# A cross-attention and expert layer on one core: projections, the gate and the turns of the output stand in other iterations

## The reference

```python
def attention(x, cross_input, ...):             # B, T, TC, C, H = 8, 512, 1024, 256, 16
    q, k, v = heads(x @ Wq + bq), heads(x @ Wk + bk), heads(x @ Wv + bv)
    att = where(causal, einsum('bhqd,bhkd->bhqk', q, k) * scale, -inf)
    y = softmax(att) @ v
    qc = heads(x @ Wcq + bcq)
    kc, vc = heads(cross_input @ Wck + bck), heads(cross_input @ Wcv + bcv)
    y = y + softmax(qc @ kc^T * scale) @ vc
    return y @ Wp + bp

def experts(x, gate_w, ...):                    # x: 4096 tokens
    scores = (tanh(x @ gate_w.T) + 1) * 0.5
    vals, idx = top_k(scores.T, 512)            # per expert
    h = gelu(einsum(layernorm(x[idx]), fc1s) + b1s)
    return x.at[idx].add((einsum(h, fc2s) + b2s) * vals)

x = x + attention(layernorm(x), ctx, ...)
x = x + experts(layernorm(x), ...)
```

## Time and profile before

| | |
|---|---|
| median of 3 runs | 1535.83 us (1532.77 to 1536.47) |
| the profiled execution | 1536.36 us, its span 1534.6 us |
| TensorE busy (matmul) | 1433.9 us, 93% |
| VectorE busy | 1167.2 us, 76% |
| ScalarE busy | 899.4 us, 59% |
| GpSimd busy | 551.7 us, 36% |
| mean granted clock of TensorE | 0.963 |
| DMA | 155.21 MB, mean 101 GB/s |

### The profile page before, as it was taken

One profiled execution on the slowest core, in us unless ns is written; L12 is line 12 of the kernel. 1 busy time (PEld: TensorE's weight loads), 2 busy tenths in 40 slices (PEclk: granted clock), 3 DMA queues, 4 the chain that ended last, 5 costly groups with the idle time before them and its releaser, 6 DMA issues. The chain is left out here.

```text
span 1534.6 us, 25472 instructions
## 1 busy us (share of the span) xinstructions
PE 1433.9 (93%) x8558; PEld 690.1 (45%) x8560; DVE 1167.2 (76%) x3025; ACT 899.4 (59%) x1753; POOL 551.7 (36%) x1015
## 2 busy tenths in 40 slices
PE   8899999999999999999999999999998947999997
PEld 4443343444344434444443444344443323766674
DVE  6879888988898888889888988898894176455441
ACT  2067777777777777777777777777777401112111
POOL 4032234341444144423534341443113122454452
PEclk9599999999999999999999999999999877999998
DMA  6884666738482947485566738392800120444442
GB/s 177 113 143 88 96 104 135 91 85 126 120 119 68 151 110 95 98 175 88 89 123 149 93 83 125 107 120 73 132 3 3 42 88 20 123 101 117 128 94 51
DMA packets 82387, 155.21 MB, mean 101 GB/s; under 512 B 13008, under 2 KB 46416, under 8 KB 82256
## 3 DMA queue, kind: packets, MB, share of 16 engines
q1 hardware_dynamic: 74752, 142.43, 49.0%
q0 software_dynamic: 6144, 8.52, 3.3%
q10 hardware_dynamic: 1360, 2.62, 0.5%
HBM read 96.52 MB, written 53.08 MB: 97 GB/s over the span
## 5 line engine op out<-in xcount | busy, mean ns | idle before, releaser
L850 ACT ACTIVATE probs<-bank_ps 128x512 f32<-128x512 f32 (+1 forms) x1408 | 721.6, 581 | 226.4 <-PE bank_ps L640 222.4
L956 DVE TENSOR_REDUCE chunk_max<-bank_ps 128x1 f32<-128x512 f32 x1024 | 652.0, 682 | 85.8 <-PE bank_ps L679 80.7
L640 PE MATMUL bank_ps<-q_stack,k_stack 64*128 64x512 f32 (+3 forms) x1536 | 507.2, 420 | 45.4 <-ACT probs L850 43.8
L679 PE MATMUL bank_ps<-k_stack,q_stack 62*128 62x512 f32 (+3 forms) x1536 | 525.4, 431 | 9.5 <-DMA k_stack<-parts 4.4
L679 PEld LDWEIGHTS bank_ps<-k_stack,q_stack 62*128 62x128 f32 x1536 | 248.4, 190 | 359.7 <-DVE chunk_max L956 235.3
L1165 POOL TENSOR_TENSOR pool_idle<-pool_idle 128x1 f32<-128x1 f32 x293 | 56.7, 194 | 757.6 <-ACT probs L850 520.7
L640 PEld LDWEIGHTS bank_ps<-q_stack,k_stack 64*128 64x128 f32 x1536 | 237.1, 187 | 128.2 <-ACT probs L850 125.2
L658 PE MATMUL out_ps<-probs,v_cross 128*32 128x512 f32 x2048 | 275.3, 610 | 0.0
L959 DVE CUSTOM_DVE_ANT_0 masked<-bank_ps,causal 128x128 bf16<-128x128 f32 (+3 forms) x512 | 232.0, 484 | 56.8 <-PE bank_ps L679 54.9
L1503 ACT ACTIVATE h<-h_ps,b1T 128x512 f32<-128x512 f32 x64 | 44.0, 687 | 226.9 <-PE h_ps L1435 224.9
L1435 PE MATMUL h_ps<-ff_yT,w1T 128*128 128x512 f32 x256 | 113.0, 595 | 0.6 <-DVE ff_yT L1516 0.6
(11 more groups left out here) (173 smaller groups left out, 1329.6 us busy)
## 6 DMA issues: line engine op xcount, KB each, us to landing
parts_dram<-parts SPq DMA_DIRECT2D x70, 512.0 KB, 2.7
k_stack<-parts_dram SPq DMA_DIRECT2D x180, 192.0 KB, 14.4
q_stack<-parts_dram SPq DMA_DIRECT2D x180, 128.0 KB, 13.3
w1T<-in_L_ffn_fc1s SPq DMA_DIRECT2D x8, 1024.0 KB, 5.6
w2T<-in_L_ffn_fc2s SPq DMA_DIRECT2D x8, 1024.0 KB, 7.4
z_rows<-z_sb SPq DMA_DIRECT2D x8, 528.0 KB, 14.3
x_sb<-in_x SPq DMA_DIRECT2D x8, 512.0 KB, 4.4
ctxT<-in_ctx SPq DMA_DIRECT2D x8, 512.0 KB, 14.1
```

What stands on the lines that cost most here:

```text
L640: mm = pe.matmul(bank_of(turn)[:, of.at:of.end], k_stack[base:base + SIDE, g, pair, of.keys:of.keys + P], q_stack[base:base + SIDE, g, pai ...
L679: return pe.matmul(bank[:, 0:n], q_stack[base:base + MAX_ROWS, g, pair, qc:qc + P], k_stack[base:base + MAX_ROWS, g, pair, k0:k0 + n], sta ...
L850: nc.scalar.activation(probs[:, buffer(u, i, p), side, columns], bank_of(("score", g, i, p, side))[:, columns], ACT.Exp, scale=SCALE)\
L956: nc.vector.tensor_reduce(dst, bank[:, 0:n], AX.X, ALU.max).then_inc(max_done, 1)
```

## The change

Two tables are changed, and nothing else: the place of twelve pieces and of seven outputs. All work is the same, and so are the loops that read the tables.

```diff
@@ PLAN, L71 @@
-    (0, 7): (("shift", 0),), (0, 8): (("k", 0),), (0, 9): (("q", 0),), (0, 10): (("kc1", 0),), (1, 1): (("qc", 0),),
-    (1, 2): (("kc0", 0),), (1, 7): (("shift", 0), ("proj0", 0)), (2, 1): (("proj1", 0),), (2, 2): (("q", 1),),
-    (2, 5): (("vc0", 0),), (2, 6): (("vc1", 0),), (2, 7): (("shift", 0),), (2, 8): (("zT0", 0),),
-    (2, 10): (("zT1", 0),), (3, 0): (("kc1", 1),), (3, 2): (("qc", 1),), (3, 3): (("k", 1),), (3, 4): (("kc0", 1),),
-    (3, 6): (("v", 0),), (3, 7): (("shift", 0),), (3, 8): (("gate", 0),),
+    (0, 7): (("shift", 0),), (0, 9): (("qc", 0),), (0, 10): (("kc1", 0),), (1, 1): (("q", 0),), (1, 2): (("k", 0),),
+    (1, 3): (("kc0", 0),), (1, 7): (("shift", 0), ("proj0", 0)), (2, 1): (("proj1", 0),), (2, 2): (("q", 1),),
+    (2, 3): (("vc1", 0),), (2, 7): (("shift", 0),), (2, 8): (("kc1", 1),), (2, 10): (("zT0", 0),),
+    (3, 0): (("vc0", 0),), (3, 2): (("qc", 1),), (3, 3): (("kc0", 1), ("zT1", 0)), (3, 4): (("k", 1),),
+    (3, 6): (("v", 0),), (3, 7): (("shift", 0), ("gate", 0)),
@@ OUTPUT_PLAN, L79 @@
-    (0, 1): ("turn_cross",), (0, 2): ("divide_cross",), (0, 6): ("turn_self",), (0, 8): ("divide_self",),
+    (0, 1): ("turn_cross",), (0, 2): ("divide_cross",), (0, 3): ("turn_self",), (0, 5): ("divide_self",),
...
-    (1, 3): ("divide_self",), (2, 1): ("turn_cross",), (2, 2): ("divide_cross",), (2, 4): ("turn_self",),
-    (2, 5): ("divide_self",), (3, 2): ("turn_back",), (3, 4): ("turn_cross",), (3, 5): ("divide_cross", "turn_self"),
-    (3, 8): ("divide_self",),
+    (1, 3): ("divide_self",), (2, 1): ("turn_cross",), (2, 2): ("divide_cross", "turn_self"),
+    (2, 8): ("divide_self",), (3, 2): ("turn_back",), (3, 3): ("turn_cross",), (3, 4): ("divide_cross",),
+    (3, 5): ("turn_self",), (3, 6): ("divide_self",),
```

## The result

| | before | after |
|---|---|---|
| median (lowest to highest) | 1534.51 us (1531.16 to 1538.76) | 1539.38 us (1533.46 to 1547.87) |
| runs, on the same chip | 20 | 20 |
| ratio, 95% interval | | 1.0036 [1.0024, 1.0047] |
| profiled execution | 1536.36 us | 1533.84 us, span 1532.1 |
| TensorE busy | 1433.9 us | 1428.4 us |

The change makes the kernel 0.36% slower, 4.9 us between the medians. The profiled execution of after happens to be one of its shortest (1533.84 where the median is 1539.38), so this trace alone would have suggested a gain. What makes a run long has therefore to be found from several profiles.

A forecast was written before the change was run, and what follows sets the result against it. TensorE, busy 93% of the span, was taken as the bound. Middle batches -1.7 us, batch 0 0, batch 7 -0.5 and batch 1's slow stretch -0.2 gave -2.4, a median of 1533.5 us; range 1528.5 to 1539.0.

The forecast's parts named there:

- (0, 8): Iteration 8 of unit 0: loses projection k, from 4.20 us to a bare slot of 2.62, -1.58 a middle batch.
- (1, 3): Iteration 3 of unit 1: bare at 2.69 us, gets kc0 and takes 3.18, +0.49 a middle batch.
- (3, 3): Iteration 3 of unit 3: gets kc0 and zT1 for k, -0.23 us a middle batch.
- (3, 7): Iteration 7 of unit 3: gate joins the shift, +1.30 us on 3.33; bank wait bounded by 0 and +0.2.
- -0.28: Sum of all slot entries in a middle batch, in us, with 0.4 either way.
- rival 2: Gate waits 0.2 for its bank, VectorE late at (2, 2), (2, 8): +0.1 to +0.3 a batch, 1536-1537 us; chance 0.2.
- Queues passed: GpSimd and SyncE queues: splits, stores and fills of moved pieces stay covered, cost 0; lost cover under 1 us a batch.
- I leave the number of falls as it is: TensorE's clock drops to its lower level at gates as often as before; one costs 1.13 us in a middle batch.
- Rival 3: Shift and gate in a row make the clock fall at (3, 7) every middle batch: 1542 us (1539.5 to 1547); chance 0.12.
- batch 0: First batch: the gate's empty turn joins the shift, +0.9 at most against 0.48 saved; about 0, within 1 us.
- -1.7: The six middle batches, 1 to 6, together: total change in us from the slot entries.
- -0.5: Batch 7: empty turns move from three slots to three, two late slots are freed; between -1.5 and +0.5 us.

The follow-up runs named there:

- h1: The changed kernel, unaltered, measured once more on another job: 1.0026 of the kernel before, 1539.07 us.
- e1: The changed kernel with the gate put back from (3, 7) to its own slot (3, 8): 1.0017 of before, 1539.56 us.
- f2: The changed kernel with the context load issued from ScalarE's queue and not SyncE's: 1.0055 of before, 1542.62 us.
- f3: The changed kernel with the context load on ScalarE's queue and the gate's matmuls 128 columns wide: 1.0024 of before, 1538.77 us.
- e4: The changed kernel with each gate matmul 128 columns wide, reading its eight columns 16 times (wide gate): 1.0014 of before, 1538.24 us.
- e2: The kernel before with only the gate moved, beside the shift in (3, 7): 1.0048 of before, 1541.64 us.
- g3: The kernel before with the gate moved beside the shift in (3, 7) and made 128 columns wide: 1.0017 of before, 1536.42 us.
- f1: The kernel before with the gate's matmuls 128 columns wide, still in (3, 8): 0.9981 of before, 1532.59 us.
- e3: The changed kernel with the first half's projections back in their old slots, k in (0, 8): 1.0033 of before, 1540.08 us.
- g4: The changed kernel with the first half's projections back in their old slots and the gate 128 columns wide: 0.9995 of before, 1534.29 us.
- f4: The kernel before with the gate cut into two halves, in bare slots (3, 1) and (3, 5): 1.0016 of before, 1536.61 us.
- h2: The changed kernel with only the residual load queued behind the shift of unit 1 (later load), gate narrow: 1.0005 of before, 1535.4 us.
- h3: The kernel before with only the residual load queued behind the shift of unit 1: 0.9993 of before, 1533.93 us.
- g1: The changed kernel with the gate 128 columns wide and the residual load queued behind the shift of unit 1: 0.9991 of before, 1533.17 us.
- g2: The kernel before with the gate 128 columns wide and the residual load queued behind the shift of unit 1: 0.9979 of before, 1531.07 us.
- h4: The changed kernel with wide gate, later residual load and the gate back in (3, 8): 0.9986 of before, 1531.4 us.

## Why the prediction was wrong

**The slots were right.** In a middle batch of after: (0, 8) 2.62 (2.62 foretold), (1, 2) +0.86 (+0.87), (1, 3) 3.27 (3.18), (2, 3) 3.30 (3.30), (2, 5) and (2, 6) 2.71 and 2.70 (2.70), (2, 8) 3.32 (3.33), (3, 4) +0.86 (+0.87), (3, 8) 2.61 (2.62). Of the small misses three add up: (1, 3) and (3, 3) are 0.09 longer than foretold, and (3, 7) is 4.89 for 4.63. I had bounded its wait for a bank by 0.2 and taken a value near 0. TensorE's timeline of after shows what came of it:

```profile
779.95 0.28 PE L705 MATMUL bank_ps<-ident,row_max 128*32 128x128 f32 x1
780.34 1.86 PEld L695 LDWEIGHTS bank_ps<-gateT,zT 128*128 128x128 f32 x16 [0.30 <-ACT probs L850]
```

The gate's first weight load waits 0.30 us for an exponential, behind the shift's transpose, which I had counted on to cover it. A middle batch without lateness came to 143.5 us against 143.45, where I had -0.28. That is near the lower end of **rival 2** (+0.1), by the wait for the bank that it named, and over six batches the miss is worth 2 us.

**The step that failed** is in "Queues passed": "I cost all this at 0". I had followed the stores and fills of the pieces that move, and left out the shift's own round trip, whose piece stays where it is. The cover of that round trip moved. The -1.58 at (0, 8), the largest gain of the sum, was taken from the time in which that round trip is hidden. The trace of before has it: stores of up to 8.98 us with some 9.5 of room. In the six profiles with (0, 8) empty and the loads ahead of the shift (after, h1, e1, f2, f3, e4) the lateness is 0.9, 1.1, 1.2, 1.8, 6.2 and 9.0 us, 3.4 in the mean. In the seven with `k` there (before, e2, g3, f1, e3, g4, f4) it is 0, 0, 0, 0.3, 0.7, 0.7 and 2.6, 0.6 in the mean. By the runs, what the later load wins more in the change than in before is 0.14% (h1 to h2, less before to h3) to 0.21% (e4 to g1, less f1 to g2), or 2 to 3 of the 4.9 us; these differences of differences have intervals wider than themselves, the gains in the change alone (0.21 and 0.23%) one of about 0.2 to either side. A typical batch doesn't show this cost: most lose nothing, and a few lose much.

**The clock** was a cost that I had called a rival. It is one in both kernels, and by most of the runs somewhat more of the changed one. The wide gate ends the falls at the gate: none at 56 gates in eight profiles (e4, f1, f3, g1 to g4, h4), where the nine profiles with the narrow gate in one piece (before, after, e1, e2, e3, f2, h1 to h3) have them at 22 of 63, one to five each: 6 of 21 with the gate in (3, 8), 16 of 42 with the gate beside the shift. Where two kernels differ in the width alone, it takes 0.19% (before to f1) and 0.14% (h3 to g2) with the gate in (3, 8). Beside the shift it takes 0.31% (e2 to g3), 0.38% (e3 to g4), 0.31% (f2 to f3) and 0.14% (h2 to g1); e4 stands 0.22% below after, 0.12% below h1. The difference of the means, 0.1%, is 1 to 2 us of the 4.9, but no more than the noise of such ratios. The granted clocks of the single runs point the same way: 0.9636 in the mean of the 32 runs of after and h1, 0.9649 in that of the 140 of before. In these sets 0.001 less goes with 0.8 to 1.3 us more, so that I estimate 1 to 2 us here too. If it is so, "I leave the number of falls as it is" is a second step that failed; its share isn't shown beyond noise. One more fall, in (3, 2) of batch 7 of h3, stands at neither place.

The clock goes with the spread as well. In the sets of before and of after the runs with the lower granted clock are the longer ones (correlations of -0.8 to -0.9), and where the wide gate and the later load stand together the runs spread over 3.1 to 4.0 us (g2, g1, h4). Rival 3 has its mechanism, as f2 shows with five falls in seven. It doesn't have its "in every middle batch", since the trace of after has one fall at a gate, and h1, the same kernel, four. That the measured time is close to the lower end of its range (1539.5) is chance. The Trainium skill (TensorE: Matmul & The Clock Gate, Part 4) says that transposes don't count as busy in the same way. The runs don't isolate that, as none moved the shift's transpose without the gate; with the wide gate directly behind it there was no fall at 35 gates.

**The rest**, 0.12% or 1.8 us between g2 and g1, has neither lateness nor gate falls in it. Part of it is the 0.05 to 0.1 us a middle batch. The other part stands in batch 0, which I had put at about 0, within 1. There the gate doesn't exist, and its turn of the bank stays empty; a score waits for VectorE's half of the shift:

```profile
206.76 0.50 PE L640 MATMUL bank_ps<-q_stack,k_stack 64*128 64x512 f32 x1 [0.47 <-DVE shift L1048]
```

Without a fall (3, 7) takes 4.30 us there for 3.33 (h1, h2), +0.97 where I had +0.9 at most. In five of the eleven profiles with the gate beside the shift the clock falls right behind this wait as well (after at 207.15 us, e3, e4, g1, g3), and the slot takes 5.06 to 5.61. None of the seven other profiles has that fall. Slots (3, 7) and (3, 8) of batch 0 together take 6.43 us in before and 7.60 in the mean of those eleven. This fall the wide gate can't prevent, as there is no gate.

**The number.** 1533.5 us was forecast and 1539.38 measured. Against the 1534.51 of before in the same comparison, the parts are: lateness 2 to 3 us, batch 0 about 1.2, the middle batches 0.3 (0.05 by 6) where I had -1.7, and batch 7 about 0 (134.0 us in g1 as in g2) where I had -0.5. Together with 1 to 2 us for the clock at the gates these are 4.5 to 6.5 us, where 4.9 were measured, and 4.0 when the same kernel was measured again (h1). How the loss divides between transfer and clock is known to no better than 1 or 2 us. Two profiles of the same kernel, after and h1, have one and four falls at a gate, so that profiles alone can't tell.

## What to carry to other kernels

Before work is moved out of a stretch, list the round trips whose latency that stretch hides, those above all whose own pieces don't move, and set their time in the trace against the room that is left; a gain in a bare slot can be a loan from a transfer. Read the whole queue ahead of an urgent transfer, with the times at which its entries land, and order large loads that nobody needs yet behind it. A profile of one execution can be among the shortest of its kernel; where runs spread by 1%, read the rare events (a slow store, a clock fall) in several.

## What was not expected of the hardware

- A matmul with 8 moving columns is hardly cheaper than one with 128, with the same weights: the slot with 16 of them takes 4.25 us (wide) against 4.16. With the wide ones TensorE's clock stayed at its upper level at all 56 gates.
- A 32 KB store can take 8 to 10.8 us from issue to landing where its median is 2.2 to 3.4 by profile, and moving one of the loads ahead of it to another engine's queue left it at 8 (f2). With the residual load moved behind it, it took 6.6 at most in g1 and 8.4 at most in h2 and h4. Fills issued 17 to 20 us ahead of it were still landing 5 to 7 us after its issue.
- The clock fell at 207.15 us, 0.4 us after a wait of 0.47 us had ended, with no matmul of few columns near it, though the shift's transpose begins 2.2 us ahead. Why that place has a fall in some executions and not in others is open.
